# Four transformer layers, float32: the second feed-forward product of the quantised layer in quarters between the next group's keys, queries and values, and masked plain scores computed in pairs

## The reference

```python
# layer 1, twice (self, then context), between layer norms
sim  = einsum('bhid,bhjd->bhij', fq(q, dq), fq(k, dk)) * SCALE
attn = softmax(sim)
out  = einsum('bhij,bhjd->bhid', fq(attn, dw), fq(v, dv)) @ wo + bo
a, g = split(h3 @ ff_w1 + ff_b1)
x    = a * gelu(g) @ ff_w2 + ff_b2 + x          # the second feed-forward product
# layer 2, both attentions; layer 3, the second
logits = einsum('bhqd,bhkd->bhqk', qh, kh) / sqrt(16) + mask
out    = softmax(logits) @ vh
```

## Time and profile before

| | us |
|---|---|
| median of 3 runs | 1988.7 |
| lowest and highest | 1986.86 and 1989.36 |
| the profiled execution, its own time | 1985.87 |
| its span in the trace | 1984.2 |

### The profile page before, as it was taken

How to read it: one execution, slowest core, us unless ns; L and a number is a source line. 1 busy time by engine, 2 the same in 40 slices (tenths; PEclk the granted TensorE clock), 3 DMA queues, 4 the chain that set the end, 5 groups by cost and what they waited for, 6 DMA issues and landing times.

```text
span 1984.2 us, 35897 instructions
## 1 busy us (share of the span) xinstructions
PE 1822.8 (92%) x13057; PEld 1396.5 (70%) x13057; DVE 1270.0 (64%) x2286; ACT 1037.5 (52%) x3078; POOL 906.9 (46%) x1209
## 2 busy tenths in 40 slices
PE   4998889899999999999999999999999999999997
PEld 4887767677777777777767677676676776766766
DVE  5899996765675575574574756756647547365471
ACT  2222224565565475475465655655545656555662
POOL 4466555564474463472353534644434333333340
PEclk8999999899999999999999999999999999999999
DMA  8200000002000000000002000000000000000000
GB/s 236 85 11 6 11 6 6 1 7 91 1 7 6 1 7 6 1 7 7 1 7 91 1 7 6 7 7 1 7 6 1 12 1 7 22 7 1 12 1 11
DMA packets 31077, 35.73 MB, mean 18 GB/s; under 512 B 3164, under 2 KB 29752, under 8 KB 30520
## 3 DMA queue, kind: packets, MB, share of 16 engines
q1 hardware_dynamic: 30904, 33.44, 5.4%
HBM read 31.34 MB, written 2.10 MB: 17 GB/s over the span
## 4 chain that ended last, share of the span: by engine, by line
PE 63%; DVE 20%; ACT 10%; issue 6%; POOL 1%; DMA 0%; SPq 0%; DVEq 0%; ACTq 0%; POOLq 0%
PE ps L596 33%; PE ps L816 6%; PE ps L746 6%; PE ps L861 4%; PE ps L827 4%; PE ps L793 3%; ACT work L996 3%; ACT work L1003 3%; DVE work L1196 3%; PE ps L768 3%; DVE xn L1050 2%; DVE rowmax L1200 2%; PE ps L609 2%; ACT hT L910 2%; DVE O L1166 1%
## 5 line engine op out<-in xcount | busy, mean ns | idle before, releaser
L596 PE MATMUL ps<-hT,w_slot 128*128 128x256 f32 x1696 | 399.6, 388 | 20.6 <-ACT hT L910 16.1
L1325 POOL TENSOR_TENSOR work<-KT,own_head 128x512 f32<-128x512 f32 x256 | 262.4, 1047 | 284.9 <-PE ps L816 179.5
L596 PEld LDWEIGHTS ps<-hT,w_slot 128*128 128x128 f32 x1696 | 315.8, 191 | 77.6 <-ACT hT L910 21.9
L1003 ACT ACTIVATE work<-work,rowmax 128x128 f32<-128x128 f32 x768 | 244.9, 392 | 168.0 <-DVE rowmax L1200 167.2
L996 ACT ACTIVATE work<-ps,rowmax,score_scale 128x128 f32<-128x128 f32 x512 | 227.0, 470 | 141.7 <-DVE rowmax L1204 140.6
L827 PEld LDWEIGHTS ps<-ident,work 128*128 128x128 f32 x1536 | 183.9, 141 | 143.8 <-issue 74.7
L816 PE MATMUL ps<-work,QT 128*128 128x512 f32 x512 | 266.5, 605 | 9.9 <-POOL work L1325 4.9
L1401 POOL TENSOR_SCALAR work<-work,winv 128x128 f32<-128x128 f32 x512 | 185.9, 383 | 144.4 <-DVE winv L1216 142.2
L827 PE MATMUL ps<-ident,work 128*128 128x128 f32 x1536 | 233.4, 275 | 19.1 <-ACT work L1003 17.0
L1239 DVE RECIPROCAL O<-ps 128x128 f32<-128x128 f32 x128 | 122.2, 954 | 174.5 <-PE ps L861 173.8
L989 ACT ACTIVATE work<-ps 128x512 f32<-128x512 f32 x256 | 150.6, 595 | 91.6 <-PE ps L827 91.4
(11 more groups left out here) (134 smaller groups left out, 3252.1 us busy)
## 6 DMA issues: line engine op xcount, KB each, us to landing
ctx_in<-in_ctx SPq DMA_DIRECT2D x32, 256.0 KB, 2.8
w_slot<-in_L_xattn_W SPq DMA_DIRECT2D x2, 1024.0 KB, 6.3
w_slot<-in_L_xattn_ff_w SPq DMA_DIRECT2D x1, 2048.0 KB, 11.5
w_slot<-in_L_xattn_ffn_w SPq DMA_DIRECT2D x2, 1024.0 KB, 9.5
w_slot<-in_L_xattn_w SPq DMA_DIRECT2D x2, 1024.0 KB, 9.5
out<-x_all SPq DMA_DIRECT2D x8, 256.0 KB, 2.1
x_all<-in_x SPq DMA_DIRECT2D x1, 1536.0 KB, 11.6
pad<-in_mask_Bx1x1xS_fk SPq DMA_DIRECT2D x1, 1024.0 KB, 5.4
```

The source lines that it names most:

```text
L596: mm = pe.matmul(dst, lhsT(k), rhs(k), start=(k == 0 and not onto), stop=(k == chunks - 1 and not more))
L1003: ex = act.activation(prob[i % NPF][:, tok(h)], src[:, tok(h)], ACT.Exp, bias=shifts[:, at:at + 1])
L1325: pool.tensor_tensor(KB[u % NK].rearrange("p (h k) -> p h k", h=HU), keys, own_head[:, e:HC:2].unsqueeze(2).broadcast_to([P, HU, S]), ALU. ...
```

## The change

Two edits. First, in `join`, for layer 1 followed by layer 1: the next group's keys, queries and values move to one, two and three spots behind `tin`, and `y2` is issued as four quarters, one at each of the four spots behind those pieces; the sum moves into the next phase's first spot. As `y2` holds bank `one` all the while, q and v of these groups (`between`) both use bank `other`: q waits for `k_ready` and v for `q_ready`. Second, in masked plain attentions (`paired`): POOL makes one spread for two units, with `own_four`, in which the first 64 rows hold heads 0 to 3 and the last 64 rows heads 4 to 7 of a feature half. TensorE does two units in one even step: four products of 64 rows by 256 columns, the two halves of the array in turn, into banks 0 and 1. The pair waits for `masked` of the unit just ahead of it. The wait for the values stands at step 1 and not in the score. `values_pair` takes each head from its new place. The diff, without blank lines:

```diff
@@ -160,6 +160,14 @@
     pieces = [(at.get(piece, y2 + spot - tin), start, piece, arg, n) for piece, spot, arg, n in first]
+    if layer == 1 and after == 1:
+        at.update({"tin": y2, "k": y2 + 1, "q": y2 + 2, "v": y2 + 3, "keys": y2 + 3})
+        pieces = [(at.get(piece, y2 + spot - tin), start, piece, arg, n) for piece, spot, arg, n in first]
+        second = [piece for piece, _, _, _ in last].index("y2")
+        pieces += [(spot, end, piece, arg, n) for piece, spot, arg, n in last[:second]]
+        pieces += [(y2 + part, end, f"y2{part}") + last[second][2:] for part in range(Y2)]
+        return pieces, [(0, tail, piece, arg, n) for piece, _, arg, n in last[second + 1:]]
     after_y2 = [piece for piece, _, _, _ in last].index("y2") + 2
@@ -276,6 +284,7 @@
         own_quad = sb("own_quad", [P, HU], BF16)
+        own_four = sb("own_four", [P, HU])
         ones_pair = sb("ones_pair", [P, 4, DH])
@@ -611,6 +620,7 @@
                     swapped = ahead or "early" in arg
+                    between = layer == 1 and g > 0 and piece in ("q", "v") and n["att"] == 0
                     if piece == "ctx":
@@ -636,13 +646,16 @@
                             pe.wait_ge(q["hT_ready"], C * due("tin", layer, g, n["tin"]))
+                        elif between:
+                            pe.wait_ge(q["k_ready"], C * (use("att", layer, g, 0) + 1))
                         else:
                             pe.wait_ge(q["yadd_done"], G * use("yadd", layer, g, n["yadd"]))
                             if st == 0 and n["yadd"]:
                                 pe.wait_ge(c[1]["yadd_done"], G * use("yadd", layer, g, 0))
                         for m in range(C):
-                            mm = product((other if swapped else one)[:, m * T:(m + 1) * T], lambda k: w[arg["w"] % "q"][:, k, m * P:(m + 1) * P],
+                            mm = product((other if swapped or between else one)[:, m * T:(m + 1) * T], lambda k: w[arg["w"] % "q"][:, k, m * P:(m + 1) * P],
                                          lambda k: source[:, k, :], C)
@@ -660,7 +673,7 @@
-                        pe.wait_ge(q["k_ready"], C * (use("att", layer, g, n["att"]) + 1))
+                        pe.wait_ge(q["q_ready" if between else "k_ready"], C * (use("att", layer, g, n["att"]) + 1))
                         for j in range(G):
@@ -784,6 +797,7 @@
                 pp = None if quant else phase("plain", layer, g, mix, st)
+                paired = not quant and "mask" in arg
                 lag = ATT_LAG[quant]
@@ -799,21 +813,32 @@
                         pe.wait_ge(q["k_ready"], C * (att + 1))
-                    if u == 1:
-                        pe.wait_ge(q["v_ready"], G * (use("att", layer, g, n["att"]) + 1))
                     if quant and u in WARM_SCORES:
                         warm(0, WARM_SCORES[u])
                     pe.wait_ge(s["KB_ready"], U * ap + u + 1)
-
-                    if u >= 2 and "mask" in arg:
-                        pe.wait_ge(s["masked"], U * masked_phase(layer, g, mix, st) + u - 1)
-                    else:
+                    if quant:
                         pe.wait_ge(s["exp_ready"], U * ap + u - 1)
-                    if quant:
                         half = slice(u % 2 * (P // 2), (u % 2 + 1) * (P // 2))
                         pe.matmul(bank(u % 2), QTb[st][half, m, tok(j)], KBb[u // 2][half, :], start=True, stop=True).then_inc(s["scores_ps"], 1)
+                        return
+                    if not paired:
+                        pe.wait_ge(s["exp_ready"], U * ap + u - 1)
+                        pe.matmul(bank(u % 2), QT[st][:, m, tok(j)], KB[u % NK], start=True, stop=True).then_inc(s["scores_ps"], 1)
+                        return
+                    if u:
+                        pe.wait_ge(s["masked"], U * masked_phase(layer, g, mix, st) + u)
                     else:
-                        pe.matmul(bank(u % 2), QT[st][:, m, tok(j)], KB[u % NK], start=True, stop=True).then_inc(s["scores_ps"], 1)
+                        pe.wait_ge(s["exp_ready"], U * ap)
+                    for part in range(2):
+                        cols = slice(part * US // 2, (part + 1) * US // 2)
+                        for e in range(2):
+                            half = slice(e * (P // 2), (e + 1) * (P // 2))
+                            mm = pe.matmul(bank(e)[:, cols], QT[st][half, m, tok(j)], KB[u // 2][half, cols], start=True, stop=True)
+                    mm.then_inc(s["scores_ps"], 2)
@@ -858,12 +883,15 @@
                                 own = ones_pair[:, 2 * e:2 * e + 2, :] if summed else V[st][:, j, m * HU + h, 2 * e:2 * e + 2, :]
-                                mm = pe.matmul(bank(4 + m)[h * 32:(h + 1) * 32, cols], own, PTF[(u + e) % 4][:, tok(h)],
+                                tile, head = (h // 2, 2 * (h % 2) + e) if paired else (e, h)
+                                mm = pe.matmul(bank(4 + m)[h * 32:(h + 1) * 32, cols], own, PTF[(u + tile) % 4][:, tok(head)],
                                                start=(e == 0), stop=(e == 1))
                     mm.then_inc(s["o_ps"], 2)
                 def step(i):
-                    if i < U:
+                    if i == 1:
+                        pe.wait_ge(q["v_ready"], G * (use("att", layer, g, n["att"]) + 1))
+                    if i < U and not (paired and i % 2):
                         scores(i)
@@ -1072,6 +1100,7 @@
                         att = use("att", layer, g, n["att"])
+                        between = g > 0 and n["att"] == 0
                         d = 4 * arg["quant"] + "qkv".index(piece)
@@ -1079,7 +1108,7 @@
                         else:
-                            dst, scratch, b = (QTb[st], QT[st], other if swapped else one) if piece == "q" else (KTb[st], KT[st], one if swapped else other)
+                            dst, scratch, b = (QTb[st], QT[st], other if swapped or between else one) if piece == "q" else (KTb[st], KT[st], one if swapped else other)
                             quantise(dst.rearrange("p c t -> p (c t)"), scratch.rearrange("p c t -> p (c t)"), b, d, at,
@@ -1306,7 +1335,7 @@
-                j, m, e = u // UJ, u % UJ // 2, u % 2
+                j, m = u // UJ, u % UJ // 2
                 if u == 0 and layer == 1 and mix == 0 and st == 0 and g == 0:
@@ -1320,11 +1349,19 @@
                     return
-                pool.wait_ge(s["scores_ps"], U * ap + u + 1 - NK)
                 keys = KT[st][:, m, tok(j)].unsqueeze(1).broadcast_to([P, HU, S])
-                pool.tensor_tensor(KB[u % NK].rearrange("p (h k) -> p h k", h=HU), keys,
-                                   own_head[:, e:HC:2].unsqueeze(2).broadcast_to([P, HU, S]), ALU.mult)\
-                    .then_inc(s["KB_ready"], 1)
+                if "mask" not in arg:
+                    e = u % 2
+                    pool.wait_ge(s["scores_ps"], U * ap + u + 1 - NK)
+                    pool.tensor_tensor(KB[u % NK].rearrange("p (h k) -> p h k", h=HU), keys,
+                                       own_head[:, e:HC:2].unsqueeze(2).broadcast_to([P, HU, S]), ALU.mult).then_inc(s["KB_ready"], 1)
+                    return
+                behind = max(u - 6, u // 2 + 1 - NK) if layer == NL - 1 else u - 6
+                pool.wait_ge(s["scores_ps"], U * ap + behind)
+                pool.tensor_tensor(KB[u // 2].rearrange("p (h k) -> p h k", h=HU), keys,
+                                   own_four[:, :].unsqueeze(2).broadcast_to([P, HU, S]), ALU.mult).then_inc(s["KB_ready"], 2)
@@ -1333,7 +1370,7 @@
                         for u in range(KEYS_AHEAD):
-                            if "quant" not in arg or u % 2 == 0:
+                            if ("quant" not in arg and "mask" not in arg) or u % 2 == 0:
                                 spread(layer, g, st, arg, n, u)
@@ -1405,7 +1442,7 @@
                     u = i + KEYS_AHEAD - 1
-                    if i > 0 and u < U and (not quant or u % 2 == 0):
+                    if i > 0 and u < U and (not (quant or "mask" in arg) or u % 2 == 0):
                         spread(layer, g, st, arg, n, u)
@@ -1426,6 +1463,7 @@
             pool.tensor_tensor(own_quad[:, :], own_head[:, 0:HU], own_head[:, HU:HC], ALU.add)
+            pool.tensor_tensor(own_four[:, :], own_head[:, 0:HU], own_head[:, HU:HC], ALU.add)
             pool.memset(neg_half[:, :], -0.5)
```

## The result

The changed kernel takes 1963.41 us (1959.55 to 1965.1), the kernel before 1988.29 on the same chip: ratio 0.9873, interval 0.9855 to 0.989. The forecast was 1960.5. The profiled execution took 1965.1 us (span 1963.4), 20.8 less than that of before.

What follows compares the result with a forecast made beforehand. TensorE, busy 92%, sets the pace on average, with VectorE close behind in light masked phases; 1985.9 less 16 (seam) and 12 (pairs) gives 1957.9, plus 2.8 to the median 1960.7, so 1960.5; range 1940 to 1980.

Steps and rivals of the forecast that it cites:

- The seam: Between groups of layer 1: quarters cover VectorE's quantisations, 1.9 us a seam, 11 for six, plus 5 from clock: 16 us.
- The clock term: Behind layer 1's seams: the four stretches at 1.2 GHz vanish, 1.4 us each, 5 us in all, bounds 0 and 7.
- Rival C: Layer 1's seam gives little, quantisations stick out from under their quarters and the clock still falls: 1974 us, chance 0.10.
- The pair on TensorE: Masked scores: the array halves overlap, a pair takes about 1.2 us, 0.5 less than before, 48 us of TensorE work.
- Rival D: Masked pairs: the array halves do not overlap in float32, a pair takes 2.0 us: 2010 us, slower than before, chance 0.09.
- The pairs against VectorE: Masked phases: VectorE becomes the bound mid-phase; scores give 10, POOL 5, less 3 for stands: 12 us, from 0 to 28.
- scores against waits: Masked phases: what faster pairs leave after waiting for both masks, mean 0.4 us in 24 phases: 10 us, bounds -5 and 20.
- POOL's spreads and the normalisation: Masked phases: half of POOL's spreads gone frees VectorE's normalisations, 0.2 us in 24 phases: 5 us, bounds 0 and 12.
- stands that bring the clock down: Masked pairs: 3 us taken off the part's 15 for stands that bring switches late or the clock down.
- the early score 1 and the late score 7: Ends of the longer masked phases, where TensorE's own feed-forward projections lie: these two scores are saved, 0.4 to 0.8 us.
- Rival B: Masked phases: pairs give nothing, the saving turns into mask waits or stands bring the lower clock: 1973 us, chance 0.24.
- Rival A: Masked phases: TensorE stays the bound and the pairs' whole 48 us arrive: 1925 us, chance 0.06.

Runs made afterwards that it cites:

- doubled spreads: Changed kernel, but POOL makes each spread of a pair's keys a second time into a buffer nobody reads: 1977.5 us, ratio 0.9959, stretch 1000.9 us.
- serial pairs: Changed kernel, but each pair is two whole score products one behind the other: 2009.0 us, stretch 1034.3; the same with both masks ahead of the maxima: 1972.3, stretch 1000.1.
- single scores: Changed kernel without the second edit, so masked scores stay as before and only layer 1's seam is changed: 1971.3 us, ratio 0.9939, stretch 997.7 us.
- the masks first: Changed kernel, but VectorE adds both masks of a pair before taking the maxima, same work: 1943.5 us, ratio 0.9791, stretch 972.5 us.
- without the division: Changed kernel, masked attentions' division replaced by a product with a constant, no reciprocal: 1941.3 us, ratio 0.9777; the same with only the seam's change: 1964.3 us.
- unused products: Six unused products ahead of the third and fourth pair of layer 3's masked phases: 1965.4 us on the changed kernel, 1953.1 with both masks ahead of the maxima.

## Why the prediction was right, and where its steps were not

**The seam**, forecast 16 us, measured 12 by the ratio and 13.5 in layer 1's trace. I took 1.9 us of idle time a seam, and 1.9 is what is gone between the start of the feed-forward product and the output projection; but the phase ahead of each seam became only 1.32 us shorter (49.8 to 48.5), 8 us for six, not 11. Of the other 0.6, 0.2 was never idle time: 16.06 is the seam with a dip, whose score takes 0.53 us (513.50 to 514.03) and 0.32 in the seam without one. The remaining 0.4 comes back behind the seam, where the third score now waits 0.27 us for ScalarE (the row at 514.03), and did not wait before. That step left out what the earlier seam would meet next. The clock term was right: the four dips vanished, and the phases that had them lost 1.3 to 1.4 us each beside that, 5.3 against 5. Rival C is out.

**The pair on TensorE** was right: I took 1.2 us, it is 1.07 to the transposes, and the switch ahead of it. Rival D's steps of 0.22 us are not there.

**The pairs against VectorE** is where a nearly right sum hides wrong terms. The stretch gives 9.2 us for the pairs, the forecast had 12; the last phase, with the dip at 1910.0, then gave 1.9 back.

| term | forecast | measured | from |
|---|---|---|---|
| scores against waits | 10 | about 4 | the rest: 9.2 - 10 + 5 |
| POOL's spreads and the normalisation | 5 | about 10 | doubled spreads, 12.4 less 2 for their dips |
| stands that bring the clock down | -3 | -5 | four dips, 1.2 to 1.6 us each |

That the sum came so near is luck: one term was more than twice too large, one half as large as it should be, and they made up for each other.

The first term is itself a difference of two large ones. The overlap of the halves gives 46 us (serial pairs, 1034.3 against 988.5), 48 with the two dips that the serial pairs have fewer, as much as the 48 of TensorE work that I wrote down. But serial pairs take 37 us more than single scores (997.7), 2.5 of them their two dips, although POOL's 10 are in their favour: doing two scores in one go costs 44. In this cost are the wait for both banks ahead of the pair and the one signal behind it, before which neither mask can start; no run takes them apart.

The step that failed is the size of what the wait for both masks leaves over: a mean of 0.4 us in each of 24 phases. Take from what each kind of phase lost what the doubled spreads give back there. Then the 39.4 us phases keep 0.7 and the 33.3 us ones 0.6, within the 0.4 to 0.8 that I had for the early score 1 and the late score 7; the 31.3 us ones keep 0.2, and the light ones nothing. The long phases' gain was right, and I spread it over phases that don't have it.

That VectorE becomes the bound in the middle of a phase is half right. Its gapless rows hold for the first part of a phase, in both kernels, and there an added 0.52 us arrives in full; in the second part VectorE stands, and three of the four reciprocals cost the phase next to nothing. What I had not seen is that in the first part not VectorE's load alone counts but its order: the pair needs both masks, the masks need the whole pair, and in the changed kernel a maximum, a reciprocal, a division and the other stream's piece stand between them. With the masks first, the same load, the overlap is worth 28 (1000.1 against 972.5), 29 without the dip, and doing two scores in one go costs 2 + 10 = 12 instead of 44. That POOL's 10 are the same there is argued, not measured.

The light phase of layer 2, which I had at 0.3, lost 0.4, and the doubled spreads take 0.52 back: all of it is POOL's. The phases of 39.4 us lost 1.5 where I had 0.8 at most, and 0.7 to 0.8 of it is POOL's too.

For the POOL term the prediction had both answers. I took 5, and 12 as the bound that goes with the exclusive lock in the Trainium skill ("SBUF — State Buffer", section SBUF: two separate sides). The measured 10 lies near that bound. The single rows agree with the rule in part: the two normalisations from 1119.07 on end at 1120.31, 0.47 us behind the spread's end at 1119.84. In the kernel before it is 0.47 too (1134.21 and 1133.74), without the division 0.48 (1112.14 and 1111.66). So the first is held until about the spread's end, but had both begun only then, their 0.72 would have ended 0.72 behind it.

**Rival B** came true in half: of the 53 us that TensorE saves 37 turned into waits for the masks, and the clock fell at new places. That the pairs gave 8 us all the same is mostly POOL's doing, in the term that I had thought the smaller. **Rival A** is out; the masks first, 1943.5, go half of the way to its 1925 with no work taken away, by the order on VectorE alone.

## What to carry to other kernels

Where two units of work share one instruction group, look first at what now stands between the last read of both buffers and the next group: put the instructions that free the buffers first on the engine that reads them, and all else behind. Before an engine is called the bound of a phase, read its gaps from end to end of it, not in a few rows: here one part of the phase had none and the other many. Take work off it: if the phase hardly moves, most of that work stood where nobody waited, and the order in the part where somebody does is worth more than the load. And when work on POOL is halved, count what VectorE runs beside it.

## What the runs showed of the hardware

Float32 products on the two row halves run side by side: the pair of 4 instructions of 512 columns takes 1.06 us, the one of 8 instructions of 256 columns 1.07, where two whole products take 1.72. Nothing was to be gained by splitting them.

Two VectorE normalisations take 0.72 us alone and 1.24 us beside a spread on POOL, and end 0.47 us behind it.

In a window of 0.1 us at the start of a pair two instructions are in flight, the second started within 0.01 us of the first, where the two of a whole product start 0.43 us apart (half of the 0.86 of a score):

```profile
1118.65 0.49 PE L840 MATMUL ps<-work,QT 64*128 64x256 f32 x2 [0.38 <-DVE work L1225]
```

A dip of the granted clock to 1.2 GHz, 3.4 us long, costs 1.2 to 1.6 us in a masked phase and 1.3 behind a seam. TensorE can be kept from it by unused products in its stands, but in the neighbouring phases, which had no dip, the same products cost 1.5 us each: it paid in neither version.
